# A decoder layer on one core: the causal term of the key scores as 32-row products in all groups, GpSimd's selects taken out, and the norm, the constants and the unread products placed anew

## What is computed

```
x = x + attn(layernorm(x))          # RWKV: 32 heads of 8 channels, chunked scan, group norm, silu gate
x = x + xattn(layernorm(x), ctx)    # 16 heads of 16 channels, causal softmax over 128 keys
x = x + ffn(layernorm(x))           # 8 experts top 2, and a shared one; hidden 176 * 8 + 704
# the part that the change touches:
scores = einsum('bhqd,bhkd->bhqk', qh, kh) / sqrt(HD)
scores = where(tril(ones), scores, finfo.min)
attn = softmax(scores, axis=-1)
```

## Time and profile before

| | us |
|---|---|
| median of three runs (630.28 to 634.41) | 632.08 |
| profiled execution | 632.54 |
| its span on the core | 630.8 |
| TensorE busy (of the span) | 588.7 (93%) |
| VectorE / ScalarE / GpSimd busy | 405.8 / 279.3 / 346.3 |
| mean granted TensorE clock | 0.989 of full |

### The profile page before, as it was taken

How to read it: one execution, slowest core, us unless ns; L and a number is a source line. 1 busy time by engine, 2 the same in 40 slices (tenths; PEclk the granted TensorE clock), 3 DMA queues, 4 the chain that set the end, 5 groups by cost and what they waited for, 6 DMA issues and landing times.

```text
span 630.8 us, 15812 instructions
## 1 busy us (share of the span) xinstructions
PE 588.7 (93%) x6435; PEld 477.8 (76%) x6435; DVE 405.8 (64%) x841; ACT 279.3 (44%) x637; POOL 346.3 (55%) x467
## 2 busy tenths in 40 slices
PE   7968877879999999999999999999999999999997
PEld 6534455544798888854798988964798999989997
DVE  5888797878763566878764566878863455752121
ACT  4845542231425655252334655343324666244332
POOL 7756124327464766524364766533364676519776
PEclk9979999998999999999999999999999999999999
DMA  8941000002131112002021111102011112117330
GB/s 190 341 114 36 0 2 2 2 1 69 17 87 35 40 44 60 31 18 69 11 83 43 41 44 59 31 18 69 10 43 42 46 48 60 30 38 131 89 57 18
DMA packets 41906, 34.18 MB, mean 54 GB/s; under 512 B 9917, under 2 KB 41286, under 8 KB 41834
## 3 DMA queue, kind: packets, MB, share of 16 engines
q1 hardware_dynamic: 39930, 31.34, 19.2%
q10 hardware_dynamic: 1904, 1.84, 0.9%
HBM read 30.98 MB, written 2.17 MB: 53 GB/s over the span
## 4 chain that ended last, share of the span: by engine, by line
PE 53%; DVE 22%; POOL 9%; ACT 7%; issue 7%; DMA 1%; POOLq 0%; SPq 0%; ACTq 0%; DVEq 0%
DVE A L1598 7%; PE bank L1059 7%; PE bank L1060 6%; PE bank L1061 6%; PE bank L1055 5%; PE bank L1098 4%; PE bank L1252 3%; PE bank L1099 3%; PE bank L1101 3%; DVE nm L1676 3%; PE bank L1179 3%; PE bank L1168 3%; POOL hb L635 2%; POOL hT L622 2%; ACT A L922 1%
## 5 line engine op out<-in xcount | busy, mean ns | idle before, releaser
L622 POOL TENSOR_TENSOR hT<-hb,hT 128x256 fp32r<-128x256 f32 (+1 forms) x102 | 78.3, 768 | 71.7 <-ACT hT L804 71.7
L635 POOL TENSOR_TENSOR hb<-hb,cwb 128x256 f32<-128x256 f32 (+1 forms) x102 | 77.3, 758 | 57.5 <-DVE hb L1573 57.1
L1573 DVE TENSOR_TENSOR hb<-hb,bank 128x256 f32<-128x256 f32 (+1 forms) x102 | 42.6, 418 | 101.0 <-ACT hb L814 101.0
L804 ACT ACTIVATE hT<-hb 128x256 fp32r<-128x256 f32 (+1 forms) x102 | 42.4, 416 | 123.8 <-POOL hb L635 121.3
L1059 PE MATMUL bank<-xTf,wGh 128*128 128x256 f32 x272 | 82.6, 304 | 0.3
L1598 DVE TENSOR_TENSOR A<-bank,decay 128x512 f32<-128x512 f32 x128 | 77.5, 680 | 7.9 <-PE bank L1168 7.8
L1061 PE MATMUL bank<-xTf,wGl 128*128 128x256 f32 x272 | 75.9, 279 | 0.0
L1060 PE MATMUL bank<-xTf,wGh 128*128 128x256 f32 x272 | 75.9, 279 | 0.0
L1060 PE MATMUL bank<-xTf,wUh 128*128 128x256 f32 x256 | 71.5, 279 | 0.0
L1059 PE MATMUL bank<-xTf,wUh 128*128 128x256 f32 x256 | 71.5, 279 | 0.0
L1061 PE MATMUL bank<-xTf,wUl 128*128 128x256 f32 x256 | 71.3, 279 | 0.0
(11 more groups left out here) (234 smaller groups left out, 1413.2 us busy)
## 6 DMA issues: line engine op xcount, KB each, us to landing
cwb<-cw_rows SPq DMA_DIRECT2D x54, 128.0 KB, 2.9
A<-cw_rows SPq DMA_DIRECT2D x18, 128.0 KB, 3.7
A<-in_x SPq DMA_DIRECT2D x4, 512.0 KB, 4.3
res<-in_x SPq DMA_DIRECT2D x4, 512.0 KB, 4.9
out_x<-res SPq DMA_DIRECT2D x8, 256.0 KB, 2.8
rawG<-in_L_ffn_w_gate SPq DMA_DIRECT2D x2, 704.0 KB, 6.5
rawU<-in_L_ffn_w_up SPq DMA_DIRECT2D x2, 704.0 KB, 6.8
cwb<-cw_rows SPq DMA_DIRECT2D x12, 112.0 KB, 2.6
```

The lines of the kernel that those rows point to most:

```text
L622: pool.tensor_tensor(low, hb[hr, c % 2, :], hT[hr, c % 2, 0, :].bitcast(F32), ALU.subtract).then_inc(h_lo, 1)
L635: pool.tensor_tensor(hb[hr, c % 2, :], hb[hr, c % 2, :], cwb[hr, c % CWS, :], ALU.mult).then_inc(h_scaled, 1)
L804: act.activation(hT[hidden(n), c % 2, 0, :], hb[hidden(n), c % 2, :], ACT.Copy).then_inc(h_hi, 1)
L1573: tt(h, h, up_part(PS[5 + c % 2], n), ALU.mult).then_inc(gu_used, 1)
```

## The change

1. `maskS` and `ahead` become one tile `fence` of 128x352 bf16. Its left part gives the term for queries on the partitions, its right part the same for keys on the partitions. A new helper `fences(b, side)` issues 16 products of 32 rows and 128 columns. `query_scores` calls it in all groups, so group 0's four full products are gone; `key_scores` calls it too, ahead of the maxima's products, so an exponential gives zero where the key is behind the query. GpSimd's 64 selects (L698) and their semaphore are gone; `attend` waits for the exponentials.
2. `fence` and `selc` (18 constants in a chain of their own, with a semaphore of their own) are made after the memsets of `xvp` in group 0. TensorE waits for the 18 before the first `query_scores`.
3. Unread products in new places: 6 before and 4 after the eighth product of group 0's `scores`, 15 before `turn_routing(0)`; in group 0's cross attention 3 in each `query_scores`, 3 and 2 around each turn of the maxima, 8 between the two `attend` of a pair.
4. VectorE: in groups 1 and 2 `layer_apply` stands ahead of the ticks of `x1c` and `x2c`.

```
-        CONSTS = HEADVAR_MADE + 1 + 3 * GB + 2 + 7 + E + 9 + 3
+        FENCES = 9 + 9
+        CONSTS = HEADVAR_MADE + 1 + 3 * GB + 2 + E + 3
...
@@ gpsimd, start @@
-            made(pool.memset(maskS[:], 0.0))
-            made(pool.affine_select(out=maskS[:], in_=maskS[:], compare_op=ALU.is_ge, fill=NEG, base=0,
-                                    pattern=[[-1, P]], channel_multiplier=1))
...
-            made(pool.memset(ahead[:], 0.0))
-            for i in range(4):
-                rows = ahead[32 * i:32 * i + 32]
-                made(pool.affine_select(out=rows, in_=rows, compare_op=ALU.is_ge, fill=NEG, base=-96,
-                                        pattern=[[1, P + 96]], channel_multiplier=-1))
-            made(pool.memset(selc[:], 0.0))
-            for base in range(0, -P, -XH):
-                made(pool.affine_select(out=selc[:], in_=selc[:], compare_op=ALU.not_equal, fill=1.0, base=base,
-                                        pattern=[[-1, XH]], channel_multiplier=1))
+            def selecting_columns():
+                fenced(pool.memset(fence[:], 0.0))
+                for i in range(4):
+                    rows = fence[32 * i:32 * i + 32]
+                    fenced(pool.affine_select(out=rows[:, 0:P], in_=rows[:, 0:P], compare_op=ALU.is_ge, fill=NEG, base=-96,
+                                              pattern=[[1, P]], channel_multiplier=-1))
+                    fenced(pool.affine_select(out=rows[:, 2 * P - 32:352], in_=rows[:, 2 * P - 32:352], compare_op=ALU.is_ge, fill=NEG, base=0,
+                                              pattern=[[-1, P]], channel_multiplier=1))
+                fenced(pool.memset(selc[:], 0.0))
+                for base in range(0, -P, -XH):
+                    fenced(pool.affine_select(out=selc[:], in_=selc[:], compare_op=ALU.not_equal, fill=1.0, base=base,
+                                            pattern=[[-1, XH]], channel_multiplier=1))
...
@@ gpsimd, group 0 after the memsets of xvp; and the selects @@
                     pool.wait_ge(xvp_rest, 2)
+                    selecting_columns()
...
-                    for i in range(4):
-                        pool.wait_ge(p_exp, g * 16 + 4 * b + i + 1)
-                        e3 = weights_of(g, b)[:, i, :].rearrange("p (h t) -> p h t", h=4)
-                        pool.affine_select(out=e3, in_=e3, compare_op=ALU.is_ge, fill=0.0, base=0,
-                                           pattern=[[0, 4], [1, T]], channel_multiplier=-1).then_inc(p_ready, 1)
...
@@ tensor @@
                         if n >= 7:
+                            if n == 7 and g == 0:
+                                idle_product(6, 4)
                             pe.wait_ge(pt_ready, g * 32 + n - 6)
...
                         elif n == 4 and g == 1:
+                            idle_product(15, cw_bank(0))
                             turn_routing(0)
...
+                    if u == 0 and g == 0:
+                        idle_product(4, 4)
                     pe.wait_ge(vpad_ready, g * 8 + u + 1)
...
+                def fences(b, side):
+                    for j in range(4):
+                        for i in range(4):
+                            rows, block, c = slice(32 * i, 32 * i + 32), slice(32 * j, 32 * j + 32), side + 96 - 32 * j
+                            mm(PS[score_base(g, b) + i].rearrange("p (h t) -> p h t", h=4)[:, :, block], fence[rows, c:c + P],
+                               identb[rows, 32 * i:32 * i + 32].unsqueeze(1).to_broadcast([32, 4, 32]), start=j == 0, stop=False,
+                               skip_group_check=True)
...
@@ query_scores @@
-                        if g == 0:
-                            mm(PS[score_base(g, b) + i][:, :], identb[:], maskS[:].unsqueeze(1).to_broadcast([P, 4, P]), start=True, stop=False,
-                               skip_group_check=True)
...
+                    if g == 0:
+                        idle_product(3, score_base(g, b) + 3)
+                    fences(b, 0)
...
@@ turn_maxima, key_scores, attend @@
+                    if g == 0:
+                        pe.wait_ge(max_ready, b + 1)
+                        idle_product(3, score_base(g, b) + 1)
                     pe.wait_ge(nm_ready, g * 4 + b + 1)
...
+                    if g == 0:
+                        idle_product(2, score_base(g, b) + 1)
                     pe.wait_ge(nmT_ready, g * 4 + b + 1)
+                    fences(b, P)
...
-                    pe.wait_ge(p_ready, g * 16 + 4 * b + 4)
+                    pe.wait_ge(p_exp, g * 16 + 4 * b + 4)
...
                 if g == 0:
+                    pe.wait_ge(fence_made, FENCES)
                     query_scores(0)
...
                         attend(b)
+                        idle_product(8, 1)
                         attend(b + 1)
...
@@ vector @@
-                        point(g, f"x{b}c")
                         if b in (1, 2) and g + 1 < NG:
                             layer_apply(0, g + 1, tokx, tokx, range(2 * b - 2, 2 * b))
+                        point(g, f"x{b}c")
```

More of the change, by code:

```diff
@@ L70, in decoder_layer @@
         wR = sb("wR", [P, KC, E + 2], F32)
-        maskS = sb("maskS", [P, P], BF16)
-        ahead = sb("ahead", [P, P + 96], BF16)
+        fence = sb("fence", [P, 352], BF16)
         selc = sb("selc", [P, XH], BF16)
@@ L1288, in query_scores @@
                             pe.wait_ge(p_exp, g * 16 + 4 * (b - 1) + i + 1)
-                        if g == 0:
-                            mm(PS[score_base(g, b) + i][:, :], identb[:], maskS[:].unsqueeze(1).to_broadcast([P, 4, P]), start=True, stop=False,
-                               skip_group_check=True)
                         if b == 0 and i == 2:
                             pe.wait_ge(q_ready, g * 2 + 2)
-                    for j in range(4):
-                        for i in range(4 if g else 0):
-                            rows, keys = slice(32 * i, 32 * i + 32), slice(32 * j, 32 * j + 32)
-                            mm(PS[score_base(g, b) + i].rearrange("p (h t) -> p h t", h=4)[:, :, keys], ahead[rows, 96 - 32 * j:96 - 32 * j + P],
-                               identb[rows, 32 * i:32 * i + 32].unsqueeze(1).to_broadcast([32, 4, 32]), start=j == 0, stop=False,
-                               skip_group_check=True)
+                    if g == 0:
+                        idle_product(3, score_base(g, b) + 3)
+                    fences(b, 0)
                     for m in range(2):
@@ L1317, in key_scores @@
                             mm(PS[score_base(g, b) + i][:, h * T:(h + 1) * T], selc[rows, 4 * i + h:4 * i + h + 1].to_broadcast([32, P]), nmT[rows, :],
-                               start=h == 0, stop=False, skip_group_check=True)
+                               start=False, stop=False, skip_group_check=True)
                     for h in range(4):
```

7 lines of the change are left out of this document (6 added, 1 removed).

## The result

The changed kernel took **622.97 us** in the median (621.89 to 624.93, 4 runs) against 631.94 (630.28 to 634.41, 4 runs) before: ratio **0.986**, interval 0.982 to 0.990, faster by 1.4%. In two later sets, beside the kernel before on the same chip, it was 622.84 and 622.94 (ratios 0.9881 [0.9859, 0.9903] and 0.9882 [0.9863, 0.9902]). The forecast was 625.9 with a range from 623.0 to 630.0: the side was right, the time lies 2.9 us under the forecast and a hair under the range.

What follows compares the result with a forecast made beforehand. TensorE bounds groups 1 to 3; VectorE's table products and short engine chains set group 0's pace. 632.5 - 3.2 - 1.8 + 0.7 + 0.5 - 2.4 + 2.9 - 3.3 = 625.9 us, range 623.0 to 630.0.

Steps and rivals of the forecast that it cites:

- Fences in groups 1 to 3, +2.9: `key_scores` in groups 1 to 3: each sequence's fence call costs TensorE 0.24 us, +2.9 us in all.
- Norm, -3.3: Groups 1 and 2: `layer_apply` ahead of the ticks moves into VectorE's idle and removes stalls before `down`, -3.3 us.
- Start, -3.2: Kernel start: constants off GpSimd's front let the `decay` cut start earlier, first `weigh` at 34.0 instead of 37.17, -3.2 us.
- the race: At the start, VectorE's last bonuses must start before GpSimd's cut and add; if lost, `weigh` gains 0 (rival: 629.1, 12%).
- Unread products in group 0's scores, -1.8: Group 0's scores: unread products fill TensorE's idle, the clock stays full and VectorE's wait of 1.85 us goes, -1.8 us.
- Constants beside the norm chain, +0.7: Group 0's norm chain: the 18 constants on GpSimd hold ten VectorE steps by some 0.07 us each, +0.7 us.
- Rival 1: Each norm step beside the constants waits out a whole select: +2.9 in place of +0.7, so 628.1 us; chance 10%.
- Group 0's cross attention, +0.5: Group 0's cross attention: unread products and fences cost time, `attend` stops waiting for selects, net +0.5 us (0 to +1.2).
- Group 1's scores, -2.4: Before `turn_routing(0)`: 15 unread products keep the clock, VectorE's idles of 0.47 and 2.00 us go, -2.4 us.
- The selects in groups 1 to 3, 0: Groups 1 to 3: removing GpSimd's selects spares TensorE no wait, as `attend` stands behind longer ticks, 0.
- 624.7 as the best case: Case 6: no cost beside the norm chain and none in group 0's cross attention, or a further wait gone; 12%.
- Rival 5: Fences don't run side by side in `key_scores`: 24 calls at 0.72 us more, +17, so 643 us; chance 4%.

Runs made afterwards that it cites:

- experiment 8: Changed kernel with each call of the key-side fences made twice: 626.53 us, ratio 0.9934 to the kernel before.
- experiment 3: Constants back at GpSimd's front in the changed kernel: 623.59 us, 0.9891; constants moved alone in the kernel before: 630.04 us, 0.9983.
- experiment 5: Changed kernel without the unread products of the score stages (6 and 4 in group 0, 15 in group 1): 623.88 us, ratio 0.9902.
- experiment 4: Changed kernel with GpSimd starting the 18 constants only after group 0's norm chain: 623.07 us, ratio 0.9874 to the kernel before.
- experiment 7: Changed kernel with GpSimd's selects put back and attend waiting for them: 625.04 us, ratio 0.9909 to the kernel before.

## Why the prediction was right, and where it was not

Two steps failed: the twelve key-side fence calls at full price, and a base execution that was slower than most. The norm's term had the right mechanism and was too small.

- **Fences in groups 1 to 3, +2.9: the step that failed.** "3 groups x 4 sequences x 0.24 = +2.9, all on TensorE" has the right length of a call, 0.22 to 0.24, and takes it that TensorE never waits there. It did, too briefly for most of these waits to be printed as idle, and the calls filled them: net +0.4 to +0.6 (experiment 8). One of them, before and then changed, `gate_up` to `down` in sequence 1 of group 3:

```profile
500.07 0.28 PE L1061 MATMUL bank<-xTf,wGl 128*128 128x256 f32 x1
500.32 0.39 PE L1098 MATMUL bank<-wDh,hT 128*128 128x256 f32 x1
```
```profile
489.49 0.28 PE L1065 MATMUL bank<-xTf,wGl 128*128 128x256 f32 x1
489.61 0.30 PE L1102 MATMUL bank<-wDh,hT 128*128 128x256 f32 x1
```

The distance is 0.25 before and 0.12 after. It is 0.23 to 0.27 in all three traces without the key-side fences, whether the norm or the constants are moved, and 0.12 in all eleven with them, the ones with the selects kept, the norm back, the constants at the front or unread products left out among them. None of those other parts closed it, then. A version with the fences as the only change was not run.
- **Norm, -3.3: mechanism right, size off.** 4.1 by the ratios, both ways. Per group it is 1.06, 0.90 and 0.16 alone where the forecast had "1.0 for sequence 2 and about 0.8 for sequence 3" and nothing at the out-projection; the check against group 3's pace then took off another 0.3, wrongly.
- **Start, -3.2: right for the pair of traces, by luck, and wrong as a gain.** 33.98 was forecast as 34.0. The kernel before had full clock from 9 to 14 us; the changed kernel's trace with full clock there has 32.77, 4.4 ahead. The first trace lost 1.2 of this to the half clock, which the forecast did not know of. What it had wrong in the other direction was VectorE, free 0.4 earlier than the 25.9 taken, and "one waits for `receptance` until 33.6": none did, `receptance` came at 32.54, behind the last bonus at 32.39. And the 3.2 was counted from an execution that had lost the race. By the runs the constants' place is worth 0.6 undone, and 0.2 (medians) to 1.1 (ratio) alone.
- **The base.** The sum stands against the profiled 632.54, with 0.5 for its distance to the median. The three sets of the experiments put the median at 630.2 to 630.4: about 2.2 us of that execution were chance, by experiment 3 for the most part the lost race.
- **Unread products in group 0's scores, -1.8: measured -1.5, for another reason.** The earlier `weigh` alone shrinks the idle to 1.04; experiment 5 found the products' effect between +0.45 and -1.5 by execution.
- **Constants beside the norm chain, +0.7: measured +0.87**, by experiment 4. I had ten steps at 0.07; it is six at 0.1 and two at 0.07 and 0.18. Rival 1 falls.
- **Group 0's cross attention, +0.5: measured +0.74** from 65.8 to 127.0. Under it lie two larger things that cancel: selects gone -1.8, by difference +2.5 for unread products and fences.
- **Group 1's scores, -2.4: measured -2.8**; experiment 5 puts 2.1 on the 15 products, the rest is the stage's own start.
- **The selects in groups 1 to 3, 0: right**, by experiment 7.
- **Sum.** Groups 1 to 3 gave 3.2 us in the first trace where the sum had 0.4. Of the difference 2.3 come from the fences and 0.9 from the norm (4.2 by the traces), less 0.4 lost in the scores between. By the two later sets the whole change is worth 7.5 us where the forecast had 6.6. So of the 2.9 us under the forecast about 0.9 are the gain and 2 the base, and the gain itself comes that near only because the start, 2 to 2.6 short of its 3.2 by the runs, makes up for most of the rest. The parts by the ratios (norm -4.1, constants -0.6, selects -1.8, scores' products -1.3, cross attention's 0, key-side fences +3.3) add up to -4.5 and not to 7.5. Most of the 3 us between is explained by experiment 8: a second call costs its full length, a first one in groups 1 to 3 does not, 2.5 against 0.4 to 0.6. What makes up the last microsecond was not taken apart; the parts need not be independent, since each was undone with the others in place.
- **Range and rivals.** Its low end, 623.0, rested on 624.7 as the best case. Executions of one kernel differ by 3 us here, and no bound had been put on the norm's term beyond -3.7 or on hidden fences. Both belonged in it, below 624.7. Rival 5 counts 24 new calls; there are 20 (16 key-side, 4 query-side in group 0), so its time would be 640 and not 643.

## What to carry to other kernels

Work added to the engine that bounds a stage costs its length only as far as no short wait behind it takes it up. Such waits show as distances between starts that are a tenth or two longer than the usual (0.25 against 0.12 here), though no idle is printed. Doubling a piece of work measures the second copy, which finds those waits already filled; the first is measured against a run without it. When a term of a sum comes from a near miss between two engines (a few hundredths of a microsecond), it is the property of one execution: ask in how many executions it happens before counting it, and take a second trace of the same kernel where one can be had. Moving an operation out of a chain helps every later wait on that chain, so follow it to the stage's last consumer, not to the first stall that vanishes. In this kernel, products that only keep the clock were worth their length where the idle was long (3.5 us). At 1 us of idle they bought steadiness, and the version without them had the shortest execution but no better median.

## What was not expected of the hardware

- The clock can fall or stay full behind one and the same idle: 1.24 us at 544 us, half clock in one trace of the changed kernel and full in the next, worth 1.4 us; 1.04 us in group 0's scores, 1.00 in one run and 0.79 in two others, worth 1.4; and at 9 to 14 us 0.66 or 1.00, worth 1.2.
- A norm step of 0.29 us grows by 0.1 beside a GpSimd select of 0.28, not by the select's length, while `low_bonus` of 0.34 waits out a cut of 2 us whole (2.1 to 2.2 us).
- The wait goes the other way too: a `receptance` that starts while VectorE runs bonuses 0.26 apart waited for the whole run and took 2.48 and 2.74 us instead of 1.1. In the kernel before, `receptance` came 0.44 us earlier in that run of bonuses, took 1.17, and VectorE waited instead.
- Sixteen 32-row products cost 0.22 to 0.24 us wherever they stood, also twice in a row on the same banks (32 in 0.46).
